# A graph attention layer on one core: two batches of edges per VectorE and ScalarE operation

## The chip, the core and the metric

One core of a Trainium2 chip runs the whole program. It has TensorE (PE; PEld is its weight load), VectorE (DVE), ScalarE (ACT), GpSimd (POOL) and SyncE (SP), each with a queue of its own that it works off in order, 16 DMA engines, the on-chip memories SBUF and PSUM, and HBM. The metric is the device time of one execution in microseconds.

## What is computed

6250 nodes with 256 channels, 100,000 edges sorted by destination, 8 heads of 32 channels. Cut to what matters:

```python
q, k, v = (feat @ W.T + b for W, b in ((Wq, bq), (Wk, bk), (Wv, bv)))      # by heads
score = clip(einsum('ehd,ehd->eh', q[dst], k[src]) / sqrt(32), -10, 10)
ex = exp(score - smax[dst]); alpha = ex / segment_sum(ex, dst)[dst]
wv = segment_sum(alpha[:, :, None] * v[src], dst)
x1 = feat + wv @ Wp.T + bp
h = layernorm(x1); h = gelu(h @ W1.T + b1) @ W2.T + b2                     # 1024 hidden
out = layernorm(feat + x1 + h)
```

## The kernel before

A prologue projects k and v of all nodes into rows in HBM (`kv_rows`), and q of the first 512. Then comes the stretch of the edges, and a tail for the last nodes.

**Edges.** A tile is 128 edges, a batch four tiles, a pair two batches (98 pairs, 196 batches). Eight batches are a turn (25 turns), and each engine runs its own `edges(turn, r, parity)`: a loop over the eight slots `i`, one batch a slot, in which the calls stand in the order of that engine's queue. Semaphores alone tie the engines together; the order is written out by hand. For batch `n`:

- POOL gathers four tiles of k and v rows by the edges' sources, one indirect DMA each (L362), into one of eight `kv` buffers, once `weight(n - 8)` has freed it (a wait on `s_ev`). In most turns one tile of slot 7 is not gathered but projected on TensorE from rows of x (`transpose_x`, `project_x`; an "x tile").
- PE, `q_rows` (L863): onehotT times the window of q rows gives q of each edge in `quad`, four PSUM banks, half of each used. It needs the products of the batch before, which free `quad`.
- DVE, `products` (L1463) and `scores` (L1470), `clip` (L1477): q times k, summed by head.
- ACT, `exponent` (L1108, L1109): exp into `bank5` and into `ev`.
- DVE, `weight` (L1483): v times exp into `ev`, two slots after its products (`weight(n - 2)` in slot n).
- PE, `sums` (L872): onehot times `ev`, added up in `bank4` over the pair.

By pair, and always in the same bank (`bank4`): ACT `stage` (L1117) copies the sums out, PE `merge` (L852) brings the four 32-row windows together, with a carry, ACT `copy_sums` (L1123) copies the result to `acc_sb`, SP `store_sums` writes it to HBM. `merge` and `copy_sums` stand one slot after `stage`. `sums` of the next pair waits for `copy_sums`. ACT also makes the transposed onehots two pairs ahead (L1094, L1099), DVE the onehots (L1449).

**Nodes.** Behind the edges run superblocks of 256 nodes, as `node_steps(turn, i)` spread over the slots of each engine: the sums' normalisation (`normalise`), `transpose_wv`, `project_out`, `residual`, norm, `transpose_h`, then one turn later `ffn1` in four parts with bias on ACT (L431), `gelu` (L436), `ffn2` in three parts, output. The gelu and the exp need different activation tables, so ACT loads one before and one after each gelu.

## Time and profile before

| | us |
|---|---|
| median of 3 runs | 1532.29 (1528.88 to 1538.81) |
| profiled execution, its own time | 1542.43 |
| its span, first to last instruction | 1540.6 |
| busy: PE / DVE / POOL / ACT | 1137.8 / 990.0 / 745.9 / 557.7 |
| POOL, 760 gathers of `kv` | 721.8 |

A span is what lies between an execution's first and last instruction. Busy time counts work, not waiting; the ends of matmuls are modelled, so a busy PE is not PE at its peak. A row of the trace names the line of the kernel, the engine and the tiles as out<-in. "idle before <-X" is how long the engine stood before this instruction, and whose update of a semaphore ended that. "issue" means that the profile shows no wait, "remote" that the update that ended the wait has no instruction near it in the profile. TensorE's granted clock is given as a share of 2.4 GHz, so 0.5 is 1.2 GHz.

### The profile page before, as it was taken

The numbers are of one execution on the slowest core, as the hardware profiler recorded it, in microseconds if no ns is written. First come the engines' busy times: TensorE is split into PE (matmuls) and PEld (weight loads), VectorE is DVE, ScalarE is ACT, GpSimd is POOL, SyncE is SP. The second block draws the span as 40 slices with busy tenths as digits, with TensorE's granted clock in tenths as the row PEclk, the third lists the DMA queues.
The fourth block names the chain that finished last, engine by engine and source line by source line (L and its number), as shares of the span: only waits on it lengthen the run. The fifth ranks groups of instructions, "written<-read, shape, count | busy, mean of one in ns | idle before, by whom it ended". The sixth has DMA issues, their size and how long they took to land.

```text
span 1540.6 us, 24484 instructions
## 1 busy us (share of the span) xinstructions
PE 1137.8 (74%) x6096; PEld 698.6 (45%) x6096; DVE 990.0 (64%) x1718; ACT 557.7 (36%) x1447; POOL 745.9 (48%) x800
## 2 busy tenths in 40 slices
PE   8924667776677688687668687788777877875887
PEld 7811234444344344444444444355444443443556
DVE  6824666675666676666566577667567666666673
ACT  2201223333234344334334344434334333333443
POOL 2364554554554554555545555445455544554400
PEclk9955668888888987888789888789788797798999
DMA  9975775765666666666656666656666665665510
GB/s 301 329 225 174 229 214 162 216 180 175 191 189 191 202 200 180 208 179 192 204 174 191 213 191 201 204 166 204 195 190 190 200 184 181 199 183 182 177 51 23
DMA packets 155387, 294.32 MB, mean 191 GB/s; under 512 B 32215, under 2 KB 92469, under 8 KB 155254
## 3 DMA queue, kind: packets, MB, share of 16 engines
q0 software_dynamic: 61856, 202.16, 43.8%
q1 hardware_dynamic: 93398, 90.90, 18.9%
q14 instruction: 112, 0.92, 0.2%
q8 instruction: 21, 0.34, 0.1%
HBM read 258.61 MB, written 34.34 MB: 190 GB/s over the span
## 4 chain that ended last, share of the span: by engine, by line
PE 26%; DVE 23%; another core or an unknown queue 23%; issue 21%; ACT 2%; DVEq 2%; SPq 2%; DMA 1%; POOL 0%; ACTq 0%; POOLq 0%
DVE score L1470 8%; DVE ev L1483 7%; PE quad L802 4%; PE bank L443 4%; PE bank L423 3%; PE quad L863 3%; PE bank L872 2%; DVE prod L1463 2%; PE bank L885 2%; DVE stats L453 1%; PE bank L852 1%; DVEq L1462 1%; PE bank L395 1%; PE bank L389 1%
## 5 line engine op out<-in xcount | busy, mean ns | idle before, releaser
L362 POOL DMA_INDIRECT kv<-kv_rows,src_sb x760 | 721.8, 950 | 658.7 <-DVE ev L1483 341.6
L1463 DVE TENSOR_TENSOR prod<-kv,quad 128x1024 f32<-128x1024 f32 x196 | 239.3, 1221 | 416.8 <-remote 333.3
L863 PE MATMUL quad<-qwin,onehotT 32*128 32x256 f32 x1568 | 167.3, 498 | 168.6 <-DVE prod L1463 107.3
L872 PE MATMUL bank<-ev,onehot 128*32 128x264 f32 x1568 | 150.2, 453 | 124.1 <-ACT acc_sb L1123 83.0
L1470 DVE TENSOR_REDUCE score<-prod 128x32 f32<-128x1024 f32 x196 | 238.0, 1214 | 2.4 <-DVE root L471 0.5
L1483 DVE TENSOR_TENSOR ev<-kv,bank 128x1024 f32<-128x1024 f32 x196 | 238.1, 1215 | 0.5 <-ACT ev L1109 0.5
L423 PE MATMUL bank<-hT,w_sb 128*128 128x256 f32 x736 | 215.3, 444 | 29.2 <-ACT hid L431 23.8
L863 PEld LDWEIGHTS quad<-qwin,onehotT 32*128 32x128 f32 x1568 | 73.2, 215 | 272.4 <-issue 177.9
L423 PEld LDWEIGHTS bank<-hT,w_sb 128*128 128x128 f32 x736 | 161.2, 225 | 76.3 <-issue 38.2
L443 PE MATMUL bank<-w_sb,hid 128*128 128x256 f32 x736 | 192.0, 414 | 0.1
L443 PEld LDWEIGHTS bank<-w_sb,hid 128*128 128x128 f32 x736 | 150.4, 210 | 29.9 <-issue 7.2
L431 ACT ACTIVATE hid<-bank,b_sb 128x256 f32<-128x256 f32 x184 | 77.1, 471 | 217.3 <-remote 126.9
L872 PEld LDWEIGHTS bank<-ev,onehot 128*32 128x32 f32 x1568 | 34.9, 116 | 199.5 <-issue 189.6
L1123 ACT ACTIVATE acc_sb<-bank 128x264 f32<-128x264 f32 x98 | 37.9, 386 | 238.3 <-remote 161.2
L852 PE MATMUL bank<-staged,place 128*128 128x264 f32 x196 | 81.9, 505 | 52.3 <-issue 30.2
L1108 ACT ACTIVATE bank<-clipped 128x32 f32<-128x32 f32 x196 | 38.5, 196 | 199.2 <-issue 125.6
L1117 ACT ACTIVATE staged<-bank 128x264 f32<-128x264 f32 x98 | 38.2, 389 | 181.5 <-remote 114.1
L852 PEld LDWEIGHTS bank<-staged,place 128*128 128x128 f32 x196 | 33.3, 213 | 91.8 <-issue 58.0
L395 PE MATMUL bank<-wp_sb,wvT 128*128 128x256 f32 x200 | 74.4, 536 | 0.0
L389 PE MATMUL bank<-bias_rows,one_rows 2*128 2x512 f32 (+1 forms) x120 | 63.6, 530 | 13.1 <-DVE x L401 12.4
L802 PE MATMUL quad<-wqkv_sb,xT_parts 128*128 128x512 f32 x288 | 66.4, 391 | 0.0
L802 PEld LDWEIGHTS quad<-wqkv_sb,xT_parts 128*128 128x128 f32 x288 | 54.3, 189 | 11.6 <-DVE xT_parts L1298 0.2
(128 smaller groups left out, 1176.3 us busy)
## 6 DMA issues: line engine op xcount, KB each, us to landing
dst_rows<-edge_dstT SPq DMA_DIRECT2D x50, 256.0 KB
qwin<-q_rows SPq DMA_DIRECT2D x392, 32.0 KB
kv_rows<-kv_out SPq DMA_DIRECT2D x24, 512.0 KB
kv<-kv_rows,src_sb POOLq DMA_INDIRECT x760
agg_rows<-acc_sb SPq DMA_DIRECT2D x98, 82.5 KB
xT_sb<-xT SPq DMA_DIRECT2D x25, 256.0 KB, 4.6
xq_sb<-xT SPq DMA_DIRECT2D x25, 256.0 KB
agg_in<-agg_rows SPq DMA_DIRECT2D x24, 264.0 KB
```

Source lines behind the costliest of these rows:

```text
L362: return nc.gpsimd.indirect_dma_start(out=rows, out_offset=None, in_=kv_dram, in_offset=bass.IndirectOffsetOnAxis(ap=index, axis=0))
L389: nc.tensor.matmul(rows, one_rows[:], bias_rows[:, cols], start=True, stop=False)
L395: last = nc.tensor.matmul(bank6[:, a * C:(a + 1) * C], wvT[:, (a * KC + k) * P:(a * KC + k + 1) * P], wp_sb[:, k * C:(k + 1) * C], start=F ...
L423: last = nc.tensor.matmul(bank[:, j * SB:(j + 1) * SB], w1_sb[:, k * HIDDEN + f * P:k * HIDDEN + (f + 1) * P], hT[:, k], start=(k == 0), s ...
L443: last = nc.tensor.matmul(bank[:, a * C:(a + 1) * C], hid[:, f, a * P:(a + 1) * P], w2_sb[:, f * C:(f + 1) * C], start=False, stop=(a == 1 ...
L802: last = nc.tensor.matmul(rows, lhsT, rhs, start=(n == 0), stop=(n == len(passes) - 1))
L852: nc.tensor.matmul(bank4[:, 0:ACC], place[:, slot % 2], staged[:, slot % 2], start=True, stop=True)\
L863: last = nc.tensor.matmul(quad[:, i, 0:C], onehotT[rows, slot // 2, cols], qwin[rows, slot // 2], start=True, stop=True)
L872: last = nc.tensor.matmul(bank4[WIN * i:WIN * (i + 1), 0:ACC], onehot[:, slot // 2, TILES * (slot % 2) + i, :], ev[:, slot % 4, i], start= ...
L1463: nc.vector.tensor_tensor(prod[:, slot % 2].rearrange("p (i c) -> p i c", c=C), kv[:, slot, :, 0:C], quad[:, :, 0:C], ALU.mult).then_inc(s ...
L1470: nc.vector.tensor_reduce(score[:, slot % 2], prod[:, slot % 2].rearrange("p (h d) -> p h d", d=HD), AX.X, ALU.add).then_inc(s_score, 1)
L1483: nc.vector.tensor_tensor(ev[:, slot % 4, :, 0:C].rearrange("p i (h d) -> p i h d", d=HD), kv[:, slot, :, C:2 * C].rearrange("p i (h d) -> ...
```

## The change

**By pair.** `quad` is used in full: `q_rows` fills it with q of eight tiles. `products`, `scores`, `clip`, `exponent` and `weight` each take a pair, with half as many instructions of twice the width. `ev` keeps its eight tiles' worth as two pairs; `prod`, `score` and `clipped`, which had two buffers of one batch, have one of a pair; `acc_sb` has two buffers instead of four. A pair's weighting frees both of its `kv` buffers, and `weight(p - 1)` stands in the slot of pair p.

**Order.** On PE `sums(p - 1)` come right behind `q_rows(p + 1)`, then a node step, then `merge(p - 1)`, in the slot of pair p. On ACT `exponent`, `stage` and `copy_sums` of pair p-1 all stand in this slot. The node chain moves one slot ahead (`normalise` 3 to 2, `project_out` 4 to 3, `residual` 5 to 4, and so on). The x tile of a turn goes to slot 1 of the next turn. The last turn has an order of its own (`last_edges`), in which the second FFN of an earlier superblock moves ahead, and the tail is reordered.

Core of the diff:

```diff
-        ev = sb("ev", [P, 4, TILES, ACC])
-        acc_sb = sb("acc_sb", [P, 4, ACC])
+        ev = sb("ev", [P, 2, PAIR_TILES, ACC])
+        acc_sb = sb("acc_sb", [P, 2, ACC])
...
-        prod = sb("prod", [P, 2, TILES * C])
+        prod = sb("prod", [P, PAIR_TILES * C])
...
                     if exists(n - SLOTS, BATCHES):
-                        pool.wait_ge(s_ev, n - SLOTS + 1)
+                        pool.wait_ge(s_ev, 4 * turn + (i // 2 - 3))
```

TensorE's `edges`:

```diff
-                for i in range(SLOTS):
-                    n = SLOTS * turn + i
-                    if exists(n + 1, BATCHES):
-                        q_rows(n + 1, (i + 1) % SLOTS, 4 * turn + (i + 1) // 2, turn + (i + 1) // SLOTS + 1)
-                    if i % 2 == 0 and exists(4 * turn + i // 2 - 2, PAIRS):
-                        merge(4 * turn + i // 2 - 2, (i // 2 + 2) % 4)
-                    if i != 5:
-                        node_steps(turn, i)
-                    if exists(n - 2, BATCHES):
-                        sums(n - 2, (i - 2) % SLOTS, 4 * turn + (i - 2) // 2)
-                    if i == 5:
-                        node_steps(turn, i)
...
+                for j in range(HALF_TURN):
+                    p = 4 * turn + j
+                    q_rows(p + 1, (j + 1) % 4, turn + (j + 1) // 4 + 1)
+                    if exists(p - 1, PAIRS):
+                        sums(p - 1, (j + 3) % 4)
+                    node_steps(turn, 2 * j)
+                    if exists(p - 1, PAIRS):
+                        merge(p - 1, j + 3)
+                    node_steps(turn, 2 * j + 1)
```

ScalarE's:

```diff
-                for i in range(SLOTS):
-                    n = SLOTS * turn + i
-                    if exists(n - 1, BATCHES):
-                        exponent(n - 1, (i - 1) % SLOTS)
-                    done = 4 * turn + i // 2 - 2
-                    if i % 2 == 0 and exists(done, PAIRS):
-                        copy_sums(done, (i // 2 + 2) % 4)
-                    if i % 2 == 0 and exists(done + 1, PAIRS):
-                        select_carry(done + 1, (i // 2 + 3) % 4)
...
-                    node_steps(turn, i)
-                    if i % 2 == 1 and exists(done + 1, PAIRS):
-                        stage(done + 1, (i // 2 + 3) % 4)
...
-                    if i % 2 == 0 and exists(4 * turn + i // 2 + 2, PAIRS):
-                        transposed_onehots(4 * turn + i // 2 + 2, (i // 2 + 2) % 4, turn + i // 4 + 1)
...
+                for j in range(HALF_TURN):
+                    p = 4 * turn + j
+                    if exists(p - 1, PAIRS):
+                        exponent(p - 1, j + 3)
+                        if j:
+                            node_steps(turn, 2 * j - 1)
+                        else:
+                            node_steps(turn - 1, 7)
+                        select_carry(p - 1, j + 3)
+                        stage(p - 1, j + 3)
+                    node_steps(turn, 2 * j)
+                    if exists(p - 1, PAIRS):
+                        copy_sums(p - 1, j + 3)
+                    late_steps(turn, 2 * j)
+                    if exists(p + 2, PAIRS):
+                        transposed_onehots(p + 2, (j + 2) % 4, turn + j // 2 + 1)
```

VectorE's:

```diff
-                for i in range(SLOTS):
-                    n = SLOTS * turn + i
-                    if exists(n - 1, BATCHES):
-                        clip(n - 1, (i - 1) % SLOTS)
-                    if exists(n, BATCHES):
-                        products(n, i, turn)
-                    if i % 2 == 0 and exists(4 * turn + i // 2, PAIRS):
-                        onehots(4 * turn + i // 2, i // 2)
-                    if exists(n - 2, BATCHES):
-                        weight(n - 2, (i - 2) % SLOTS)
-                    node_steps(turn, i)
-                    if exists(n, BATCHES):
-                        scores(n, i)
...
+                for j in range(HALF_TURN):
+                    p = 4 * turn + j
+                    if exists(p - 1, PAIRS):
+                        clip(p - 1)
+                    products(p, j, turn)
+                    onehots(p, j)
+                    if exists(p - 1, PAIRS):
+                        weight(p - 1, (j + 3) % 4)
+                    node_steps(turn, 2 * j)
+                    scores(p)
+                    node_steps(turn, 2 * j + 1)
```

`onehots(p)` waits for `exponent(p - 1)`, before as after. `late_steps` are the gelu (third pair of a turn) and `norm_h` (fourth).

How the queues read now. First ScalarE (ACT), from one `staged` copy to the second exponential after it, in the second and third slot of a turn (L431 is the FFN bias, L1132 the copy of projected q). Before:

```order
L1117 ACTIVATE staged<-bank 128x264
L1108 ACTIVATE bank<-clipped 128x32
L1109 ACTIVATE ev<-clipped 128x4x8
L1123 ACTIVATE acc_sb<-bank 128x264
L1126 ACTIVATE place<-carry_all 128x1
L1132 ACTIVATE q_next<-bank 128x512
L431 ACTIVATE hid<-bank,b_sb 128x256 x2
L1094 ACTIVATE distance<-dst_rows,minus_start 128x256
L1099 ACTIVATE onehotT<-distance,one_col 128x256
L1108 ACTIVATE bank<-clipped 128x32
L1109 ACTIVATE ev<-clipped 128x4x8
```

The same place now (L1162 is `stage`, L1168 `copy_sums`, L1153 and L1155 `exponent`, L448 the bias, L402 the copy of wvT):

```order
L1162 ACTIVATE staged<-bank 128x264
L402 ACTIVATE wvT<-bank 128x512
L448 ACTIVATE hid<-bank,b_sb 128x256 x2
L1168 ACTIVATE acc_sb<-bank 128x264
L1138 ACTIVATE distance<-dst_rows,minus_start 128x256
L1143 ACTIVATE onehotT<-distance,one_col 128x256
L1153 ACTIVATE bank<-clipped 128x64
L1155 ACTIVATE ev<-clipped 128x8x8
```

An exponential of one batch stood between `staged` and `acc_sb`; now none does, and the next one, for a whole pair, stands behind `acc_sb` and the transposed onehots.

Second, TensorE (PE) in the same slots (L389 and L885 project q, L423 is a quarter of the first FFN, L380 transposes wv). Before:

```order
L852 MATMUL bank<-staged,place 128x264
L423 MATMUL bank<-hT,w_sb 128x256 x4
L872 MATMUL bank<-ev,onehot 32x264 x4
L863 MATMUL quad<-qwin,onehotT 128x256 x4
L423 MATMUL bank<-hT,w_sb 128x256 x4
L389 MATMUL bank<-bias_rows,one_rows 128x256
L885 MATMUL bank<-wqkv_in,xq_sb 128x256 x2
L389 MATMUL bank<-bias_rows,one_rows 128x256
L885 MATMUL bank<-wqkv_in,xq_sb 128x256 x2
L872 MATMUL bank<-ev,onehot 32x264 x4
L863 MATMUL quad<-qwin,onehotT 128x256 x4
L852 MATMUL bank<-staged,place 128x264
```

Now, one pair (L880 is `q_rows`, L893 `sums`, L869 `merge`, L397 the transposes of wv, L440 the first FFN):

```order
L880 MATMUL quad<-qwin,onehotT 128x256 x8
L893 MATMUL bank<-ev,onehot 32x264 x8
L397 MATMUL bank<-ident,wv 128x128 x4
L440 MATMUL bank<-hT,w_sb 128x256 x4
L869 MATMUL bank<-staged,place 128x264
```

The sums of a pair stood behind a node step, and its merge behind the next q rows; now the sums stand at once behind the q rows, and a node step stands between them and their merge.

## Rows read from the trace of the kernel before

**Rows 1.** The page: span; busy us, share, instructions per engine.

```profile
span 1540.6 us, 24484 instructions
...
PE 1137.8 (74%) x6096; PEld 698.6 (45%) x6096; DVE 990.0 (64%) x1718; ACT 557.7 (36%) x1447; POOL 745.9 (48%) x800
```

**Rows 2.** Instructions on tile prod: ns min/median/max, first to last start.

```profile
L1463 DVE TENSOR_TENSOR prod<-kv,quad x196: 1214/1221/1224, 89.2 to 1479.7; 128x1024 f32<-128x1024 f32 x196
```

**Rows 3.** The waits: us in total, times, longest us.

```profile
POOL kv L362 <- DVE ev L1483: 341.6, 81, 9.1
DVE prod L1463 <- remote: 333.3, 75, 12.2
...
ACT acc_sb L1123 <- remote: 161.2, 31, 7.7
```

**Rows 4.** Timeline, 1351 to 1367 us: start, us, instruction, [idle before <-releaser].

```profile
1351.60 1.21 DVE L1483 TENSOR_TENSOR ev<-kv,bank 128x1024 f32<-128x1024 f32 x1
...
1353.59 0.94 POOL L362 DMA_INDIRECT kv<-kv_rows,src_sb  x1 [4.95 <-DVE ev L1483]
...
1355.18 0.66 PE L872 MATMUL bank<-ev,onehot 128*32 128x264 f32 x8
...
1355.90 0.39 ACT L1117 ACTIVATE staged<-bank 128x264 f32<-128x264 f32 x1 [0.35 <-PE bank L872]
...
1357.31 0.71 PE L852 MATMUL bank<-staged,place 128*128 128x264 f32 x2
...
1357.86 1.89 PE L423 MATMUL bank<-hT,w_sb 128*128 128x256 f32 x8
...
1362.61 0.95 POOL L362 DMA_INDIRECT kv<-kv_rows,src_sb  x1 [0.30 <-issue]
...
1363.77 1.22 DVE L1463 TENSOR_TENSOR prod<-kv,quad 128x1024 f32<-128x1024 f32 x1 [3.73 <-remote]
...
1365.32 0.39 ACT L1123 ACTIVATE acc_sb<-bank 128x264 f32<-128x264 f32 x1 [6.78 <-remote]
```

**Rows 5.** Groups of instructions: count, busy us, mean ns, idle us before <-releasers.

```profile
L362 POOL DMA_INDIRECT kv<-kv_rows,src_sb x760 | 721.8, 950 | 658.7 <-DVE ev L1483 341.6 <-issue 310.5 <-DMA kv_rows<-kv_out 6.6
...
L431 ACT ACTIVATE hid<-bank,b_sb 128x256 f32<-128x256 f32 x184 | 77.1, 471 | 217.3 <-remote 126.9 <-PE bank L423 65.3 <-issue 25.1
...
L1099 ACT ACTIVATE onehotT<-distance,one_col 128x256 f32<-128x256 f32 x98 | 49.8, 508 | 10.1 <-ACT distance L1094 1.4 <-issue 0.6
L1094 ACT ACTIVATE distance<-dst_rows,minus_start 128x256 f32<-128x256 int32 x98 | 49.5, 505 | 0.2
L436 ACT ACTIVATE hid<-hid 128x2048 f32<-128x2048 f32 (+1 forms) x24 | 44.2, 1840 | 0.3
L1109 ACT ACTIVATE ev<-clipped 128x32 f32<-128x32 f32 x196 | 42.0, 214 | 0.0
L1449 DVE TENSOR_TENSOR onehot<-dloc,bank 128x256 f32<-128x256 f32 x98 | 40.6, 415 | 3.8 <-ACT ev L1109 1.5 <-remote 1.5 <-issue 0.8
L1108 ACT ACTIVATE bank<-clipped 128x32 f32<-128x32 f32 x196 | 38.5, 196 | 199.2 <-issue 125.6 <-DVE ev L1483 73.3
...
L1123 ACT ACTIVATE acc_sb<-bank 128x264 f32<-128x264 f32 x98 | 37.9, 386 | 238.3 <-remote 161.2 <-PE bank L852 58.0 <-issue 19.0
...
L436 ACT ACT_TABLE_LOAD x23 | 29.5, 1283 | 0.4
...
L475 ACT ACTIVATE hn<-x,root 128x256 f32<-128x256 f32 x50 | 27.1, 589 | 4.4 <-DVE root L471 3.3 <-issue 0.7 <-DVE root L470 0.3
...
L401 DVE TENSOR_TENSOR x<-bank,x_in 128x512 f32<-128x512 f32 x24 | 16.5, 689 | 36.1 <-remote 18.1 <-issue 12.9 <-PE bank L395 5.0
```

**Rows 6.** Windows: us, busy per engine (PE to POOL), granted clock, DMA, GB/s.

```profile
640.00:697.00 57.00, 45.43 (x258) 27.31 (x257) 39.57 (x65) 24.27 (x65) 30.42 (x33) 0.88 0.65 194
80.00:136.00 56.00, 16.41 (x69) 7.79 (x73) 16.36 (x21) 4.87 (x16) 34.90 (x37) 0.51 0.66 197
```

**Rows 7.** Timeline after the edges, 1485 to 1500 us.

```profile
1490.97 7.17 PE L443 MATMUL quad<-w_sb,hid 128*128 128x256 f32 x32
```

More of the change, by code:

```diff
@@ L34 @@
 X_TILE = TILES - 1
-X_COPIED = {5: 3, 7: 6}
+EARLY_WORK, TURN_WORK = 1, 3
 EX_COL = 0
@@ L51, in configure @@
     LOOP_FROM = 6 if LOOPED else TURNS - 1
-    X_TILES = [(turn, i) for turn in range(TURNS) for i in x_slots(turn)]
+    X_FROM = 4 if LOOPED else TURNS
+    X_TILES = [x_target(turn, first) for turn in range(TURNS) for first in x_work(turn)]
     EDGE_COLS = BATCHES * TILES
@@ L68, in kv_halves, with x_work, x_target @@
     return 1 if u * SB + P >= NODES else 2
+def x_work(turn):
+    if not isinstance(turn, int) or X_FROM <= turn < LOOP_FROM + 2 * LOOPED:
+        return (TURN_WORK,)
+    return (EARLY_WORK, TURN_WORK) if turn < 2 else ()
+def x_target(turn, first):
+    return (turn, 7) if first == EARLY_WORK else (turn + 1, 1)
 def x_slots(turn):
-    if not isinstance(turn, int) or LOOP_FROM <= turn < LOOP_FROM + 2 * LOOPED:
-        return (7,)
-    return (5, 7) if turn < 2 else ()
+    if not isinstance(turn, int):
+        return (1,)
+    return tuple(i for t, i in X_TILES if t == turn)
 def x_index(turn, i):
@@ L647, in edges @@
                     n = SLOTS * turn + i
-                    done = 4 * turn + i // 2 - 2
+                    done = 4 * turn + i // 2 - 1
                     if i == 0 and exists(turn - 1, Q_UNITS - EARLY_Q):
@@ new lines, in last_edges @@
+            def last_edges(turn):
+                p, a, b = 4 * turn, turn - 2, turn - 1
+                q_rows(p + 1, 1, turn + 1)
+                ffn1(a, 0)
+                sums(p - 1, 3)
+                if exists(a - 1, SUPERBLOCKS):
+                    pe.wait_ge(f_z, a)
+                ffn1(a, 1, bank6)
+                merge(p - 1, 3)
+                pe.wait_ge(f_ev, 4 * a + 1)
+                ffn1_pair(2).then_inc(f_f1, 1)
+                sums(p, 0)
+                ffn1(a, 3)
+                merge(p, 0)
+                sums(p + 1, 1)
+                pe.wait_ge(f_ev, 4 * a + 2)
+                transpose_wv(b)
+                merge(p + 1, 1)
+                project_out(b)
+                pe.wait_ge(s_w2, 32)
+                pe.wait_ge(f_half, 1)
+                pe.wait_ge(f_x2, b + 1)
+                ffn2_part(range(FC // 2))
+                pe.wait_ge(f_gelu, a + 1)
+                ffn2_part(range(FC // 2, FC)).then_inc(f_f2, 1)
+                transpose_h(b)
@@ L1196, in node_steps @@
             def node_steps(turn, i):
-                ends = isinstance(turn, int) and turn == TURNS - 1
-                for j in x_slots(turn):
-                    if i == X_COPIED[j]:
-                        copy_x_kv(turn, j)
-                if i == 2 and exists(turn, Q_UNITS - EARLY_Q):
+                for first in x_work(turn):
+                    if i == first + 2:
+                        copy_x_kv(turn, first)
+                if i == 1 and exists(turn, Q_UNITS - EARLY_Q):
                     copy_q(turn)
-                if i + 4 in x_slots(turn):
-                    copy_x_rows(turn, i + 4)
@@ L1205, in node_steps @@
-                if i + 3 in x_slots(turn):
-                    copy_x_columns(turn, i + 3)
+                if i == 2 and exists(turn - 1, SUPERBLOCKS):
+                    copy_wv(turn - 1)
                 if i <= 3 and exists(turn - 2, SUPERBLOCKS):
                     ffn1_bias(turn - 2, i)
-                if i == 3 and exists(turn - 1, SUPERBLOCKS):
-                    copy_wv(turn - 1)
-                if i == 4 and not ends and exists(turn - 2, SUPERBLOCKS):
-                    gelu(turn - 2)
@@ new lines, in weight @@
+            def weight(p, slot, halves=(0, 1)):
+                first, last = halves[0], halves[-1] + 1
+                tiles = slice(first * TILES, last * TILES)
+                dve.wait_ge(s_exp, p + 1 + first)
+                nc.vector.tensor_tensor(ev[:, slot % 2, tiles, 0:C].rearrange("p i (h d) -> p i h d", d=HD),
+                                        kv[:, 2 * slot + first:2 * slot + last, :, C:2 * C]
+                                        .rearrange("p a i (h d) -> p (a i) h d", d=HD),
+                                        bank5[:, EX_COL + tiles.start * H:EX_COL + tiles.stop * H]
+                                        .rearrange("p (i h) -> p i h", h=H)
+                                        .unsqueeze(3).broadcast_to([P, tiles.stop - tiles.start, H, HD]),
```

383 lines of the change are left out of this document (234 added, 149 removed).

## The prediction

> **What bounds the kernel now.** I read the page first: no engine is full, TensorE is busy for 74% of the span and the clock is mostly granted [rows 1]. So the order of the handshakes sets the time, and the edge stretch is nearly all of it: the 196 `prod` products start between 89.2 and 1479.7 us [rows 2], 7.13 us apart, which is 57.05 us for a turn of eight batches and 14.3 us for a pair.
>
> Next the waits. VectorE stands 333.3 us before `prod` and ScalarE 161.2 us before `acc_sb`, both released by "remote", and POOL 341.6 us for the weighting on VectorE [rows 3]. "Remote" is a wait whose releaser the profile does not find near it. The timeline tells what it is [rows 4]. There the weighting of 1351.60 ends at 1352.81 and frees a buffer; POOL starts gathering 0.78 us later and issues eight gathers in a row, until 1363.56. Inside this burst TensorE ends two pieces that somebody waits for. The sums end at 1355.84, 2.25 us into the burst, and ScalarE's `staged` copy starts 0.06 us later. The merge ends at 1358.02, 4.43 us into the burst, and `acc_sb`, which waits for it (and for a store long past), starts at 1365.32, 7.3 us later and 1.76 us after the last gather. The product that starts at 1363.77 after a remote wait has waited for q rows in the same way. So I read: **a completion of TensorE passes early in a burst of gathers, and from about 3 us into it is held until 1 to 2 us after its end.** Where a chain crosses such a hold, gathering sets the time: 10 us of eight gathers, 1.76 us of release, then what VectorE must do until it frees buffers again. Two batches of the kernel before do this: 0.8 + 10.0 + 1.8 + a product and a weighting (1.1 + 1.2, overlapped) make 14.9, against the 14.3 measured.
>
> **The change, part by part.**
>
> *Fewer, larger VectorE operations.* Products, reductions and weightings go from 588 of 1024 elements to 294 of 2048. 512 elements take 0.689 us and 1024 take 1.215 to 1.221 [rows 2, 5], a slope of 1.03 ns an element, so 0.16 us is fixed: the double one takes 2.27 us and 294 x 0.16 = 48 us of busy time go. 98 clips go too, at the same fixed 0.16 us (my estimate for them): 16 us. VectorE waits 333 us before its products alone, so as long as something else sets the period, both are worth nothing. The Trainium skill has the rule for this (VectorE: DVE Perf Modes, on the TRN2 errata): the extra latency is paid per instruction, so one large tile pays it once. By that rule alone the kernel gains; the trace agrees with the fixed part, and what it would make of the time is a rival below.
>
> *ScalarE's exponentials* lose 98 pairs of 0.2 us; ScalarE is 36% busy: nothing.
>
> *TensorE* has the same matmuls. Nothing.
>
> *Gathers.* The same 760, but a pair's two batches are freed by one weighting, so each burst is eight gathers (seven with the x tile): 0.95 us and 0.30 us between them [rows 4, 5], 10.0 us for eight in [rows 4]. POOL alone then allows 10.0 + 0.8 = 10.8 us a pair.
>
> *The loop that closes.* Before, the weighting of a pair's second batch leads to its sums, `staged`, the merge one slot later and `acc_sb`; the next weighting that stands behind this `acc_sb` on ScalarE's queue is about three batches (21 us) on. Now sums, `staged`, merge and `acc_sb` of pair p-1 all stand ahead of the exponential of pair p, and the weighting of pair p needs that. One pair is the whole way round, with two completions of TensorE in it, and it starts with the same event that starts the burst. Queued behind the waiting `acc_sb` on ScalarE are the transposed onehots and the exponential; VectorE waits for that with its onehots and the weighting, POOL for the weighting, SP for `acc_sb` to store it.
>
> When the merge is held, weighting to `acc_sb` is 0.78 + 10.0 + 1.76 = 12.5 us, as [rows 4] have it. From there: `acc_sb` 0.39, distance 0.51, onehotT 0.51 and gaps, 1.5 together; exponentials 0.20 + 0.21 and a little for the double width, 0.5; onehots 0.41; the double weighting 2.27. That is 4.7, and the pair takes **17.2 us**. What the node steps put between on ScalarE comes on top [rows 5]: in the first pair of a turn a bias pair of 0.94 us half of the time, in the second the same always, in the third the gelu with two table loads (1.28 + 1.84 + 1.28 = 4.4), in the fourth `hn` (1.2). Held pairs: 17.6, 18.1, 21.6, 18.4.
>
> When it is not held, POOL's 10.8 us rules (VectorE needs 3 x 2.27 + 0.41 and its node steps, about 9), and in the third pair the gelu: 2.6 + 4.7 + 4.4 = 11.7.
>
> *Is it held?* The merge stands behind the sums and behind one node step. At full clock sums of eight tiles take 1.3 us (twice the 0.66 of [rows 4]), a quarter of the first FFN 1.89, the merge 0.71. From the weighting's end the merge is done after about 3.7 us in the first pair (2.9 into the burst, the edge of what passes; I take 0.6 for held), 4.6 in the second, where the transposed wv come first (3.8 into it; 0.9), 2.6 in the third (1.8; 0.3, since at half clock it would be 3 or more) and 4.8 in the fourth, with six matmuls of the second FFN at the pace of the first (4.0; 0.85). A mean share of 0.66.
>
> Sum of a turn: (0.6 x 17.6 + 0.4 x 10.8) + (0.9 x 18.1 + 0.1 x 10.8) + (0.3 x 21.6 + 0.7 x 11.7) + (0.85 x 18.4 + 0.15 x 10.8) = 14.9 + 17.4 + 14.7 + 17.3 = 64.3, less 1.0 for the burst of seven: 63.3. That is 6.2 more than 57.05, and 24 turns make **+150 us**.
>
> Bounds: with every merge held 75.7 - 1.3 = 74.4 us a turn, +416; with none 42.9, -340. In between a turn is about 42.9 + 31.5 x share, which meets 57.05 at a share of 0.45.
>
> *The clock* leans on the share. In 80 to 136 us, where TensorE is busy 16.4 of 56 us, it is granted 0.51, that is 1.2 GHz nearly throughout; in 640 to 697, busy 45.4 of 57, 0.88 [rows 6]. A held pair leaves TensorE idle for some 9 us, then the FFN piece starts at 1.2 GHz, takes twice 1.89 us, and the merge behind it is surely held. The Trainium skill says so too (TensorE: Matmul & The Clock Gate, in the table of why this matters for a kernel): an idle TensorE falls back to its half-rate clock. By it the share goes towards 1 and the time towards the upper bound; I keep 0.66, since TensorE stands for 6 us and more before this change too, and the window of 640 still has 0.88.
>
> *The tail.* The second FFN of superblock s-2, 7.17 us alone on the chain at 1490.97 [rows 7], moves in front of the last sums' follow-ups, where a part lies under VectorE's work: -7 us at the most likely, between -15 and +5, as the rest of the tail keeps its matmuls. The node chain one slot sooner has room both ways: nothing.
>
> Total: +150 - 7 = +143 on the profiled execution's own 1542.4 us (span 1540.6): 1685. The median of the runs is 10 us below that execution, so **1675 us**.
>
> **The rivals.**
>
> *A, chance 0.45, the forecast:* a share of 0.5 to 0.8, 1565 to 1790 us, most likely 1675.
>
> *B, nearly every merge held, 0.10:* cold clock, share over 0.8: 1790 to 1940.
>
> *C, faster, 0.26: the merges get out ahead of the gathers.* The place is the 3 us after a weighting, the price 6 to 10 us a pair, and the point from which it decides is the share of 0.45. For it: sums are now at once behind the weighting, and [rows 4] show a completion passing at 2.25 us; against it: every place but one has more than 2.5 us of TensorE work ahead of the merge. A share of 0.3 gives 52.4 us a turn, 24 x -4.7 = -112, less 7 and 10: 1413 us. Down to 0.2, 1340.
>
> *D, 0.10: only the operations' own fixed time counts.* If VectorE's queue sets the pace after all and the holds cost what they cost before, 48 + 16 us go and the tail's 7: 1460. It is the skill's rule from above. Against it speaks that VectorE idles for a third of the stretch.
>
> *E, even, 0.09:* a share near 0.45.
>
> **The numbers.** What a measurement of this kernel can tell from no change is about 1%. Slower by over 1%: A and B, 0.55. Within 1%: E, 0.09. Faster: C and D, 0.36. The likeliest case's own range is 1565 to 1790. The range for 8 in 10 takes in most of B and of C and all of D: 1400 to 1860.
>
> **What the profile after would show.** If right: `prod` starts further apart than 14.3 us a pair; bursts of eight gathers with 5 to 7 us of idle POOL between; ScalarE's wait before `acc_sb` by "remote" grown from 161 us to over 400, VectorE's large wait now before the onehots or the weighting and not before `prod`; a lower granted clock. If C: `acc_sb` starts within 4 us of the weighting's end in most pairs, POOL is hardly idle, and a pair takes 11 to 13 us. The forecast is wrong if holds depend on something other than the burst, or if the merge is done sooner than I count.

## The result, and the profile after

The changed kernel takes 1666.99 us (median of 4 runs, 1648.96 to 1700.14), the kernel before 1535.55 (4 runs, 1528.88 to 1554.32): 131 us more. The ratio, of fast executions alone (1649 and 1650 us against 1529 to 1539), is 1.076, 95% interval 1.067 to 1.084, or 116 us; the profiled execution below is the slowest of the four, so the main readings are set beside run 9, another profiled execution of the same kernel that took 1617 us. The forecast was 1675 us.

The profiled execution of the changed kernel has a span of 1698.3 us, 157.7 more than the one before [rows 1]. The page, its span and busy times:

```profile
span 1698.3 us, 22878 instructions
...
PE 1192.2 (70%) x6110; PEld 748.2 (44%) x6110; DVE 950.5 (56%) x1330; ACT 538.7 (32%) x1259; POOL 751.9 (44%) x800
```

VectorE is busy for 40 us less. TensorE is busy for 54 us more with nearly the same matmuls, since its clock is lower (below). Every engine's share has fallen: all wait more. The tile `prod` tells where (compare [rows 2]):

```profile
L1543 DVE TENSOR_TENSOR prod<-kv,quad x99: 1214/2287/2290, 95.2 to 1632.5; 128x2048 f32<-128x2048 f32 x97, 128x1024 f32<-128x1024 f32 x2
```

First to last product was 1390.5 us and is 1537.3: 146.8 of the 157.7 us lie in the edge stretch. Its start adds 6.0 us (95.2 against 89.2), the tail behind the last product 4.9 (65.8 against 60.9). Run 9 has the same start and tail (95.6 and 65.5) and 1454.2 us between its first and last product.

The waits (compare [rows 3]):

```profile
POOL kv L379 <- DVE ev L1569: 522.8, 60, 17.2
ACT staged L1162 <- remote: 302.5, 36, 15.7
...
DVE onehot L1526 <- ACT ev L1155: 272.4, 52, 10.3
DVE prod L1543 <- remote: 189.6, 28, 25.5
ACT q_next L1177 <- remote: 156.1, 17, 25.0
...
ACT acc_sb L1168 <- remote: 65.6, 18, 6.3
```

VectorE's wait before its products has shrunk from 333 to 190 us, and one of 272 us has come before the onehots, for ScalarE's exponential. But on ScalarE the wait by "remote" stands before `staged`, which needs the sums, and before `q_next`, which needs the projected q rows, and hardly before `acc_sb`, where I had put it. Run 9 has the same order: 210 us by "remote" before `staged`, 104 before `q_next`, 87 before `acc_sb`, 166 before `prod`, and 222 before the onehots. One held pair, the fourth of a turn, to be read against [rows 4] (start, us, instruction, idle before it):

```profile
650.66 2.28 DVE L1569 TENSOR_TENSOR ev<-kv,bank 128x2048 f32<-128x2048 f32 x1
...
653.09 1.10 PE L893 MATMUL bank<-ev,onehot 128*32 128x264 f32 x16 [1.16 <-issue]
...
653.73 0.95 POOL L379 DMA_INDIRECT kv<-kv_rows,src_sb  x1 [1.34 <-issue]
...
662.49 0.95 POOL L379 DMA_INDIRECT kv<-kv_rows,src_sb  x1 [0.30 <-issue]
...
665.44 2.29 DVE L1543 TENSOR_TENSOR prod<-kv,quad 128x2048 f32<-128x2048 f32 x1 [7.42 <-remote]
665.60 0.39 ACT L1162 ACTIVATE staged<-bank 128x264 f32<-128x264 f32 x1 [14.84 <-remote]
...
667.40 0.39 ACT L1168 ACTIVATE acc_sb<-bank 128x264 f32<-128x264 f32 x1 [1.42 <-PE bank L869]
```

The sums end at 654.19, 0.46 us into a burst of eight gathers that followed another after a pause of only 1.3 us; `staged` starts 11.4 us later, 2.2 us after the last gather. So early pieces are held too, here behind a short pause. And there is something that I had not seen in the trace of before. Another place, 28 us on, in a row of fifteen gathers (673.64 to 692.14):

```profile
682.65 0.11 PEld L893 LDWEIGHTS bank<-ev,onehot 128*32 128x32 f32 x1 [1.04 <-issue]
...
685.83 0.60 PE L893 MATMUL bank<-ev,onehot 128*32 128x264 f32 x1 [1.77 <-issue]
...
687.96 0.60 PE L893 MATMUL bank<-ev,onehot 128*32 128x264 f32 x1 [1.53 <-issue]
...
690.10 0.60 PE L893 MATMUL bank<-ev,onehot 128*32 128x264 f32 x1 [1.54 <-issue]
...
695.02 1.92 PE L893 MATMUL bank<-ev,onehot 128*32 128x264 f32 x10 [0.83 <-issue]
695.03 0.56 PEld L893 LDWEIGHTS bank<-ev,onehot 128*32 128x32 f32 x8 [0.61 <-issue]
695.04 0.60 ACT L1177 ACTIVATE q_next<-bank 128x512 f32<-128x512 f32 x1 [15.36 <-remote]
```

All inputs are there (the weighting ended at 682.54), yet TensorE gets through its first six matmuls one by one, up to 2.2 us apart, and runs the last ten within 1.9 us, from 2.9 us after the last gather on. Here not only its completions are late: it hardly gets to its next instruction.

From the trace I took, for pairs 8 to 91, the distance between the ends of successive weightings, and how long after a weighting `acc_sb` starts (over 8 us: held). The pairs of a turn are counted as in the prediction: the transposes of wv stand before the merge in the second, and the gelu behind `acc_sb` in the third.

| pair of a turn | period, forecast | measured | run 9 | held share, forecast | measured | run 9 | held / other pair, us |
|---|---|---|---|---|---|---|---|
| first | 14.9 | 13.1 | 12.7 | 0.60 | 0.29 | 0.38 | 19.7 / 10.4 |
| second | 17.4 | 19.4 | 18.5 | 0.90 | 0.86 | 0.76 | 20.7 / 11.3 |
| third | 14.7 | 15.6 | 13.9 | 0.30 | 0.33 | 0.14 | 21.6 / 12.6 |
| fourth | 17.3 | 15.6 | 14.5 | 0.85 | 0.76 | 0.57 | 17.1 / 10.9 |
| turn | 63.3 | 63.6 | 59.6 | 0.66 | 0.56 | 0.46 | |

The turn came out as forecast, and so did the order of its parts, except for the first pair, which is held half as often as I had put it. In run 9 there are fewer held pairs and the turn is 4 us shorter.

### The profile page after: what moved, and what is told of

The parts are those of the page before. It is cut to its first block and busy times, and to the rows that moved or that the text cites. A ratio compares the mean times of both kernels' runs of the same rounds, so it can differ in the third digit from the quotient of the medians.

```text
span 1698.3 us, 22878 instructions
## 1 busy us (share of the span) xinstructions
PE 1192.2 (70%) x6110; PEld 748.2 (44%) x6110; DVE 950.5 (56%) x1330; ACT 538.7 (32%) x1259; POOL 751.9 (44%) x800
## 5 line engine op out<-in xcount | busy, mean ns | idle before, releaser
L1543 DVE TENSOR_TENSOR prod<-kv,quad 128x2048 f32<-128x2048 f32 (+1 forms) x99 | 224.1, 2264 | 218.8 <-remote 189.6
L893 PE MATMUL bank<-ev,onehot 128*32 128x264 f32 x1568 | 201.7, 468 | 186.6 <-issue 134.8
L1526 DVE TENSOR_TENSOR onehot<-dloc,bank 128x256 f32<-128x256 f32 x98 | 41.3, 421 | 381.5 <-ACT ev L1155 272.4
L440 PE MATMUL bank<-hT,w_sb 128*128 128x256 f32 x736 | 220.1, 449 | 11.0 <-issue 10.1
L460 PE MATMUL bank<-w_sb,hid 128*128 128x256 f32 x768 | 219.3, 438 | 8.9 <-issue 8.3
L1569 DVE TENSOR_TENSOR ev<-kv,bank 128x2048 f32<-128x2048 f32 (+1 forms) x99 | 223.6, 2259 | 2.4 <-ACT ev L1155 2.4
L1553 DVE TENSOR_REDUCE score<-prod 128x64 f32<-128x2048 f32 (+1 forms) x99 | 223.5, 2257 | 0.8
L893 PEld LDWEIGHTS bank<-ev,onehot 128*32 128x32 f32 x1568 | 63.9, 121 | 301.1 <-issue 287.5
L440 PEld LDWEIGHTS bank<-hT,w_sb 128*128 128x128 f32 x736 | 164.8, 232 | 61.3 <-issue 29.5
L869 PE MATMUL bank<-staged,place 128*128 128x264 f32 x196 | 77.6, 484 | 139.1 <-ACT staged L1162 101.2
L1162 ACT ACTIVATE staged<-bank 128x264 f32<-128x264 f32 x98 | 38.3, 391 | 425.8 <-remote 302.5
L880 PE MATMUL quad<-qwin,onehotT 32*128 32x256 f32 x1568 | 127.9, 442 | 64.5 <-DVE prod L1543 25.8
L448 ACT ACTIVATE hid<-bank,b_sb 128x256 f32<-128x256 f32 x184 | 77.2, 471 | 231.6 <-PE bank L440 121.3
L880 PEld LDWEIGHTS quad<-qwin,onehotT 32*128 32x128 f32 x1568 | 79.7, 205 | 102.1 <-issue 97.8
L869 PEld LDWEIGHTS bank<-staged,place 128*128 128x128 f32 x196 | 39.8, 226 | 160.4 <-ACT staged L1162 112.6
L1168 ACT ACTIVATE acc_sb<-bank 128x264 f32<-128x264 f32 x98 | 38.3, 391 | 114.7 <-remote 65.6
L923 PE MATMUL bank<-wqkv_in,xgT 128*128 128x512 f32 x96 | 71.6, 887 | 0.0
L406 PEld LDWEIGHTS bank<-bias_rows,one_rows 2*128 2x128 f32 x123 | 25.7, 209 | 96.3 <-issue 74.6
```

Source lines behind the costliest of these rows:

```text
L406: nc.tensor.matmul(rows, one_rows[:], bias_rows[:, cols], start=True, stop=False)
L440: last = nc.tensor.matmul(bank[:, j * SB:(j + 1) * SB], w1_sb[:, k * HIDDEN + f * P:k * HIDDEN + (f + 1) * P], hT[:, k], start=(k == 0), s ...
L448: last = nc.scalar.activation(hid[:, f], bank[:, j * SB:(j + 1) * SB], ACT.Identity, bias=b1_sb[:, f:f + 1])
L460: last = nc.tensor.matmul(bank[:, a * C:(a + 1) * C], hid[:, f, a * P:(a + 1) * P], w2_sb[:, f * C:(f + 1) * C], start=False, stop=(a == 1 ...
L869: nc.tensor.matmul(bank4[:, 0:ACC], place[:, slot % 2], staged[:, slot % 2], start=True, stop=True)\
L880: last = nc.tensor.matmul(quad[:, i, odd * C:(odd + 1) * C], onehotT[rows, slot, odd * P:(odd + 1) * P], qwin[rows, slot], start=True, sto ...
```

## The experiments

The kernels ran in four groups, each on one chip with the kernel before between them. In two groups (chips numbered 3 and 1) it took 1509 and 1528 us, like in the result above: **condition A**. In the other two (numbered 14 and, later, 1 again) it took 1118 and 1120 us: **condition B**. Within a group the runs of the kernel before lie within 2.3% under A and 0.5% under B. Each kernel is compared with the kernel before of its own group.

**1. The merge out of the loop (A).**

```
 TensorE, pair p:                       ScalarE, pair p:
   q_rows(p + 1, ...)                     exponent(p - 1)
+  merge(p - 2, ...)                   +  copy_sums(p - 2)
   sums(p - 1, ...)                       stage(p - 1), node_steps(turn, 2 * j)
   node_steps(turn, 2 * j)             -  copy_sums(p - 1)
-  merge(p - 1, ...)                      transposed_onehots(p + 2)
```

> The change with one part undone: TensorE's merge and ScalarE's acc_sb copy of pair p-1 go back to the next pair's slot (merge(p-2) stands right behind the q rows, the copy right behind the exponential); everything else stays, the pairwise operations too. Theory 1 (holds close the loop): the loop from weighting to weighting then contains one completion of TensorE, that of the sums, which comes 1.2 to 2.1 us after the weighting and passes; the pairs that took 18 us and more mostly go, a pair takes 12.5 to 14.5 us, and the time is 1380 to 1560 us. Theory 2 (the time went into TensorE's instructions and the clock, not into the order): within 2% of 1667 us. Theory 3 (ScalarE's wait for the projected q rows, 156 us in the changed kernel, is the loss): at most 30 us faster than 1667.

Measured: 1699.0 us (4 runs), before 1528.1; ratio 1.116 (1.104 to 1.127). A pair takes 15.8 us, as in the changed kernel (15.9). Theory 1 misses by 139 us. The time lies in theory 2's range (within 2% of 1667), though runs 3 and 4 speak against TensorE's own work as the cause. The waits of this kernel:

```profile
DVE onehot L1530 <- ACT ev L1158: 358.2, 56, 11.8
ACT acc_sb L1171 <- PE bank L871: 303.1, 76, 7.7
...
ACT staged L1165 <- remote: 257.6, 49, 8.9
```

The sums' completion is still in the loop and is itself held, and the merge, now behind the q rows, has become a wait of its own. So this is no clean opening of the loop; it shows only that moving the merge alone gains nothing.

**2. The merge right behind the sums (A).**

```
 TensorE:                               ScalarE:
   sums(p - 1, (j + 3) % 4)               stage(p - 1, j + 3)
+  merge(p - 1, j + 3)                 +  copy_sums(p - 1, j + 3)
   node_steps(turn, 2 * j)                node_steps(turn, 2 * j)
-  merge(p - 1, j + 3)                 -  copy_sums(p - 1, j + 3)
```

> The changed kernel with the merge right behind its sums on TensorE (the node step behind it, not between) and the acc_sb copy right behind the staged copy on ScalarE. TensorE now idles about 1 us a pair for the staged copy, 97 us in all if nothing else moves. Theory 1 (what decides is whether the merge gets out before the burst of gathers): the merge ends 2.7 to 3.3 us after the weighting instead of 4.5 or later, fewer pairs are held, a turn falls from 63.6 to about 55 us, the time to 1420 to 1530 us. Theory 2 (completions are held wherever they fall in a burst, or TensorE gets its instructions slowly during one): 1640 to 1700 us. Theory 3 (no holds, TensorE's own time): up to 97 us slower, 1760.

Measured: 1751.9 us (4 runs, 1718.1 to 1791.6), before 1528.1: slower than the changed kernel. The second pair of a turn did what was hoped (merge 3.3 us after the weighting, 11.2 us a pair); the third, fourth and first took 18.6, 14.2 and 21.3. With that merge out early the loss came back in the pairs behind it: pairs of 16 us or more went from 37 to 42 of 84. By its time alone this fits theory 3 (up to 1760), but ScalarE's wait by "remote" before `staged`, 305 us, speaks for holds, and so for theory 2, whose range it misses by 52 us.

**3 and 4. Half the gathers, in both kernels (A).**

```
-  for t in range(tiles):                 # the four tiles of a batch
+  for t in range(tiles if turn == 0 else min(tiles, 2)):
       gather_rows(...)
```

> The changed kernel with two gathers per batch instead of four (from the second turn on; tiles 2 and 3 of a batch keep the rows of the first turn, so the result is not the reference's). A burst is four gathers, 5 us, not eight, 10 us. Theory 1 (a burst holds TensorE until 1 to 2 us after its end): a held pair is 0.8 + 5.0 + 1.1 + 4.7 = 11.6 us, the others 9 to 10, so about 10.5 x 97 + 160 = 1180 us, 1100 to 1260. Theory 2 (the chain of the operations itself, clock included, sets the pair): a pair stays at 15.9 us, 1600 us or more. Theory 3 (POOL's issue time is the bound): 10.8 x 0.5 = 5.5 us less a pair, 1130, but then POOL would be hardly idle.

> The same in the kernel before: two gathers per batch instead of four. Theory 1: bursts are shorter, the holds too, and VectorE becomes the bound at about 10 us a pair (990 us busy in all): 1080 to 1200 us. Then the changed kernel with half the gathers should be up to 64 us faster than this one (98 pairs x 4 fixed times of 0.16 us), since with short bursts the loop of one pair no longer costs. If the loop costs even without long holds, it stays slower than this one. Theory 2 (gathers are hidden): 1500 us or more.

Measured: the changed kernel 1254.0 us (2 runs), the kernel before 1120.5 (2 runs), ratios to the full kernel before 0.825 (0.815 to 0.835) and 0.737 (0.730 to 0.745). Engines' busy times, the changed kernel with half the gathers first, then the kernel before with half:

```profile
PE 1014.8 (81%) x6110; PEld 684.5 (54%) x6110; DVE 947.4 (75%) x1330; ACT 537.6 (43%) x1259; POOL 419.1 (33%) x449
```

```profile
PE 980.2 (88%) x6096; PEld 621.1 (55%) x6096; DVE 983.2 (88%) x1718; ACT 557.0 (50%) x1447; POOL 412.0 (37%) x446
```

Both kernels lose some 400 us with the gathers, more than the 330 us for which POOL is less busy, and TensorE has the same matmuls: gathering in bursts is what holds. But the gap between the two kernels stays, 133 us against 131, where fixed times alone would have made the changed one faster. The kernel before now gathers two at a time, and VectorE and TensorE are each busy for 88% of its span; the changed one gathers four at a time. I compared the end of each TensorE instruction that signals, inside a row of gathers less than 0.6 us apart, with the record of its semaphore's update, where there is one:

| kernel, condition | gathers in the row | late by, mean | over 1 us |
|---|---|---|---|
| before, half, A | 2 | 0.10 us | 2% |
| changed, half, A | 4 | 0.88 us | 37% |
| before, A | 4 | 1.3 us | 49% |
| before, A | 8 | 3.6 us | 68% |
| changed, A | 8 | 3.5 us | 68% |
| changed, order of run 5, B | 8 and more | 0.02 us | 0% |

At eight in a row both kernels are alike; but the kernel before has 52 rows of four and 40 of eight, the changed one 56 of eight, 13 of seven, ten of fifteen and none of four.

VectorE's and ScalarE's completions came 0.01 to 0.02 us late in all of them.

**5. The exponential ahead of the staged copy (B).**

```
 ScalarE, pair p:
   exponent(p - 1)
-  node_steps(turn, 2 * j - 1)
-  stage(p - 1), node_steps(turn, 2 * j), copy_sums(p - 1), late_steps(turn, 2 * j)
+  stage(p - 2), node_steps(turn, 2 * j - 2), copy_sums(p - 2), late_steps(turn, 2 * j - 2)
   transposed_onehots(p + 2)
+  node_steps(turn, 2 * j - 1)
```

> The changed kernel with ScalarE's exponential of pair p put ahead of its staged copy of pair p-1 (staged, the bias pairs and acc_sb follow it; the q copy follows too). The loop from one weighting to the next then contains no completion of TensorE on ScalarE's queue; they have one pair of slack, as before the change. All else is the changed kernel's, but TensorE's merge comes about 1 to 2 us later after its sums. Theory 1 (the closed loop through ScalarE is the loss): VectorE's wait for the exponential, 272 us, falls below 60, a pair takes 12.5 to 14.5 us instead of 15.9, the time is 1380 to 1560 us. Theory 2 (bursts of eight gathers hold TensorE longer than bursts of four, whatever the order): the wait moves to the products for q rows, a pair stays at 15 to 16.5 us, 1600 to 1700 us.

Measured: 1153.4 us (4 runs), the kernel before 1117.8; ratio 1.032 (1.029 to 1.035). The condition had changed, so the theories' ranges do not apply. What this run says is in comparison with the next two.

**6. The same with half the gathers (B).** The edits of 5 and of 3 together.

> The same order with two gathers per batch instead of four, so that the result is not the reference's. The changed kernel took 1254 us so, the kernel before 1121. Theory 1 (what is left with short bursts is the latency of the loop of one pair): 1050 to 1120 us, VectorE the bound at 9.1 us a pair. Theory 2 (the double operations or the clock cost it): 1200 to 1260 us.

Measured: 1150.3 us (2 runs), ratio 1.029 (1.024 to 1.033). Here half the gathers are worth 3 us, where under A they were worth over 400.

**7. Half the bytes (B).**

```
-  gather_rows(kv[:, i, t, :], ...)       # 2 KB a row
+  gather_rows(kv[:, i, t, 0:C], ...)     # 1 KB a row, from a table of 1 KB rows
```

> The changed kernel with gathers that fetch 1 KB for each row instead of 2 KB from the second turn on (as many gathers, half the bytes; the result is not the reference's). Theory 1 (the holds go with POOL's issuing of gathers): bursts last the same 10 us, holds too, 1560 to 1690 us. Theory 2 (the holds go with the bytes that the DMA engines still have to move): the holds shrink by half or more, 1180 to 1400 us.

Measured: 1151.9 us (2 runs), ratio 1.030 (1.027 to 1.033). Whether bytes or POOL's issuing hold TensorE can't be told where nothing is held, so that stays open. But this kernel is the changed one in all but the bytes, and it shows the sums and their `staged` copy, here of the third pair of a turn, without holds:

```profile
642.63 2.28 DVE L1569 TENSOR_TENSOR ev<-kv,bank 128x2048 f32<-128x2048 f32 x1
...
645.28 1.10 PE L893 MATMUL bank<-ev,onehot 128*32 128x264 f32 x16
...
645.69 0.94 POOL L379 DMA_INDIRECT kv<-kv_rows,src_sb  x1 [0.61 <-issue]
...
646.45 0.39 ACT L1162 ACTIVATE staged<-bank 128x264 f32<-128x264 f32 x1 [0.90 <-PE bank L893]
...
646.94 0.94 POOL L379 DMA_INDIRECT kv<-kv_rows,src_sb  x1 [0.30 <-issue]
```

`staged` starts 0.07 us after the sums, with POOL gathering almost without a break. A pair takes 10.2 us, the four of a turn 9.1, 9.4, 11.8 and 10.4.

In 5, VectorE's wait for the exponential (85.1 us in run 7) was gone. Of its three longest waits the one for the gathers is in run 7 too (29.7 us); those for `y_out` and the q rows are new:

```profile
DVE z L466 <- ACT y_out L492: 61.4, 21, 6.4
DVE prod L1552 <- DMA kv<-kv_rows,src_sb: 31.4, 5, 14.4
DVE prod L1552 <- PE quad L882: 31.1, 20, 3.3
```

**8. POOL stopped in mid-burst (B).**

```
+  if i % 2 == 1 and t == 0:
+      pool.wait_ge(s_mrg, ...)   # the merge of the pair that freed the buffers
   gather_rows(...)
```

> The changed kernel, with POOL stopped in the middle of each burst of eight: after four gathers it waits for the merge's completion of the pair whose weighting freed the buffers. Theory 1 (TensorE's completions are held while POOL gathers and released 1 to 2 us after): the merge gets out at the latest 0.8 + 5.0 + 1.1 = 6.9 us after the weighting instead of 12.5, the burst ends at 12, a pair takes 12.5 to 14 us, 1370 to 1520 us. Theory 2 (gathering time is what is missing, or completions are late for another reason): the idle POOL time is lost, 1680 to 1900 us.

Measured: 1169.4 us (5 runs), ratio 1.044 (1.042 to 1.047). Without holds the stop only costs.

**9. The changed kernel again (A).** No edit.

> The changed kernel once more, unaltered, because the four runs before this one came from a chip on which the kernel before takes 1118 us and not 1530, and on which TensorE's completions inside a burst of gathers came 0.02 us after their instructions. If the chip of this run is one where the kernel before takes about 1530 us: theory 1 expects 1630 to 1710 us and completions that come late. If it is one where it takes about 1118 us: by theory 1 (the loss of 132 us is the price of held completions) most of the loss is gone, and by the two kernels with less gathered data that ran there the changed kernel takes 1145 to 1165 us, 27 to 47 us more than before, all of it the loop's own latency (VectorE's wait of 85 us for the exponential).

Measured: 1639.6 us (4 runs), before 1509.4; ratio 1.075 (1.064 to 1.085), and completions inside rows of eight gathers 3.0 us late in the mean, 65% by over 1 us. Another group, the same picture.

**10. The exponential first, `y_out` early (A).**

```
   exponent(p - 1, j + 3)
+  if j == 0: norm_out(turn - 2)          # taken out of node_steps(turn - 1, 7)
   stage(p - 2, j + 2), ...               # the rest as in 5
```

> The order with the exponential first, and in addition ScalarE's second normalisation (y_out) put right behind the exponential that opens a turn, since VectorE waited 61 us for it there. Meant to beat both kernels. Where completions are not held: 1153 less up to 61 us, 1090 to 1130 us, against 1118 of the kernel before. Where they are held (kernel before about 1530): if the loop through ScalarE is the loss, 1380 to 1560 us; if the eight gathers in a row are, whatever the order, 1600 to 1700 us.

Measured: 1667.6 us (4 runs), before 1509.4; ratio 1.103 (1.095 to 1.111), in the group of run 9, which took 1639.6. The exponential no longer waits behind `staged` and `acc_sb`, and nothing is gained. VectorE's waits:

```profile
DVE prod L1554 <- remote: 412.2, 62, 25.2
DVE prod L1554 <- PE quad L882: 146.4, 13, 18.5
```

Before the onehots there is none left among the large ones; all of it stands before the products, for q rows. One burst's end in this kernel:

```profile
692.65 1.15 PE L882 MATMUL quad<-qwin,onehotT 32*128 32x256 f32 x16
...
699.26 0.95 POOL L379 DMA_INDIRECT kv<-kv_rows,src_sb  x1 [0.30 <-issue]
701.90 2.29 DVE L1554 TENSOR_TENSOR prod<-kv,quad 128x2048 f32<-128x2048 f32 x1 [5.91 <-remote]
...
704.10 0.41 DVE L1537 TENSOR_TENSOR onehot<-dloc,bank 128x256 f32<-128x256 f32 x1
...
704.43 2.28 DVE L1580 TENSOR_TENSOR ev<-kv,bank 128x2048 f32<-128x2048 f32 x1
...
707.50 0.94 POOL L379 DMA_INDIRECT kv<-kv_rows,src_sb  x1 [7.29 <-DVE ev L1580]
```

Last gather's end to release 1.7 us, then double product, onehots and double weighting, 4.8, then 0.8 to the first gather: 7.3 us of idle POOL, and with 10.0 us for eight gathers 17.3 us. The third and fourth pair of a turn take 16.6 and 17.0 here. The q rows that this product waits for were made at 692.65 to 693.80, with no wait of TensorE just before them, and the product started only at 701.90.

**11 and 12. The stop again, and the weighting split in two.** Meant for A, both fell into B.

> The changed kernel with POOL stopped after four gathers of each eight until the merge of the pair whose weighting freed the buffers is complete. It cost time on the chip where completions are not held (1169 us there, the kernel before 1118). Where they are held (kernel before 1510 to 1530, the changed kernel 1640 to 1667): theory 1 (the loss is the time that completions stand behind eight gathers in a row) expects the merge out at the latest 6.9 us after the weighting, 12.5 to 14 us a pair, 1370 to 1520 us. Theory 2 (POOL's lost gathering time adds to the pair): 1680 to 1900 us. On a chip without holds: 1160 to 1180 us again.

```
-  one weighting of the pair, 2048 elements
+  weight(p, slot, (0,)); weight(p, slot, (1,))    # 1024 each, each frees its batch
```

> The changed kernel with one part undone: each pair's weighting is two operations of 1024 elements again, each of which frees its batch's four buffers (products, sums, q rows and exponentials stay pairwise). The first gather of a burst starts 1.1 us sooner. Where completions are held: a held pair is VectorE's double product, onehots and weighting after the release and 12.6 us of burst and release before it, 17.6 us in all; if that is the chain, half to two thirds of the 97 pairs get 1.1 us shorter, 50 to 70 us in all, so 1570 to 1620 us, 3 to 4% below the changed kernel; if buffers are not what a pair waits for, 1640 to 1670 us. Where they are not held: 98 more fixed times of 0.16 us on VectorE, 1150 to 1170 us.

Measured: 1172.1 us (4 runs; ratio 1.047, 1.043 to 1.051), the first stop's time again, and 1154.2 us (4 runs; 1.029, 1.026 to 1.033). What they do where completions are held is not known.

No kernel of these that does the whole computation beats the kernel before, under A or B.

## Why the prediction was right, and where it was not

**That gathering holds TensorE: right, shown.** Under A, halving the gathers took 1667 to 1254 us and 1528 to 1121; under B it was worth 3 us (runs 5 and 6). But it is not the program alone that does it: under B the same rows of gathers hold nothing. What makes A or B is open; the chip's number does not tell, since 1 showed both.

**The size of a pair: right.** Held pairs were put at 17.6, 18.1, 21.6 and 18.4 us and take 19.7, 20.7, 21.6 and 17.1. Pairs that are not held were put at 42.9 us a turn; run 7, where none is, takes 40.7. The formula gives 60.5 us a turn for the measured share of 0.56, against 63.6, and 57.4 for run 9's 0.46, against 59.6.

**Which pairs are held: right for three of four.** The second, third and fourth pair came close to their shares; the first was put at 0.60 and is 0.29. The periods are off by -1.8, +2.0, +0.9 and -1.7 us, which nearly cancels: that the turn is off by only 0.3 us is luck, and in run 9 it is off by 3.7.

**What holds them: wrong in part.** The step said that the sums pass and that the merge's age in the burst, with an edge at about 3 us, decides. In the trace of before this edge is there. In the changed kernel nearly half of the early completions are late too. TensorE's completions inside rows of seven or eight gathers, those late by over 1 us, by the row's age when they were due:

| age | before | changed | run 9 |
|---|---|---|---|
| under 2 us | 5 of 56 | 40 of 84 | 38 of 96 |
| 2 to 3 us | 18 of 32 | 14 of 18 | 12 of 21 |
| over 3 us | 137 of 143 | 94 of 106 | 110 of 121 |

So of 47 held pairs 32 had `staged` start over 8 us after the weighting, before the merge could begin, and in only 15 did `acc_sb` start over 2 us behind the merge. Two terms were missing. ScalarE copies the projected q rows ahead of the second pair's `staged`, and that completion was held too (156 us in 17 waits, over 3 us in 14 of the 18 held second pairs); I had counted only bias pairs there. And I took each burst as starting afresh, where it goes with the pause before it: of the 25 bursts that began less than 2.5 us after the last gather, 24 gave a pair of 16 us or more, of the other 59 only 13 (run 9: 20 of 26, and 7 of 58). Of the 25 short pauses 15 stand in second pairs, but the others show it too (9 of 10). A pair that is not held leaves no pause: 25 of 37 such pairs are followed by a long one. No run changed the pause alone, so that it is the cause is not shown.

**The loop through ScalarE, as the cause of the loss: failed.** The step said that the next weighting must now wait for the merge and `acc_sb` of the last one, and that this closes a loop that was open before. The waits did move as it said (onehots 3.8 to 382 us idle, `prod` by "remote" 333 to 190). But with ScalarE's part opened the time did not fall (run 10: 1668 against 1640), and the loss then stood before `prod`, for q rows that were held themselves. Moving the merge did not help either (runs 1 and 2, 1699 and 1752), though these are no clean test. What the runs suggest is that under A each pair needs some completion of TensorE inside the burst, and that it hardly matters which.

**What stands in its place.** Part is shown: the changed kernel frees the buffers of eight gathers at once and the one before of four, and the longer the row of gathers, the later TensorE's completions (table in runs 3 and 4; with rows of two next to nothing is late, and the kernel before with half its gathers takes under A what the full one takes under B, 1121 and 1118 us). The changed kernel with half its gathers, in rows of four, takes 1254 us under A, about 100 more than its nearest kernels take under B. The rest is worked out, not shown: after a release VectorE must now do 4.8 us before the next buffer is free (run 10), where a single product and weighting were 2.4 [rows 2, 4], 2.4 us more in each held pair; with 0.56 of 97 pairs that is 130 us, with run 9's 0.46 it is 107. That takes the number of held pairs as unchanged, which no run shows, and with the 34 us below it comes to more than the loss. Splitting the weighting would have tested it, and fell into condition B. So what share of the loss each of the two has stays open.

**What is left without holds.** Under B the changed kernel itself was not run; runs 7 and 12, each but one step from it, take 1152 and 1154 us, 3% over the kernel before. There VectorE waits 85 us for the exponential (run 7), more than the 40 us that its operations save. So by these two, some 34 of the 131 us have nothing to do with held completions. Opening the loop there exchanged that wait for others and gained nothing (run 5), so this cause is narrowed down, not settled.

**The fixed time of an operation** was right (2.29 us, the median of a double product, 2.27 forecast), and worth nothing, as forecast: VectorE's busy time fell by 40 us, less than the 64 that I had counted. **The clock** fell a little, not to the floor: over the middle of the edge stretch 0.80 against 0.84, and 0.83 in run 9.

```profile
300.00:1500.00 1200.00, 858.61 (x4455) 525.94 (x4454) 678.33 (x894) 404.18 (x947) 560.83 (x590) 0.80 0.58 171
```

**The tail** was put at -7 us and is +4.9. The second FFN starts 16.2 us after the last product (11.3 before) and runs alone, as in [rows 7]. The step that failed is that it would move in front: in the last turn's order the transposes of wv and the projection now stand between the last sums and it. The projection ran at half clock, 3.78 us against 1.99 before, and run 9 shows the same:

```profile
1643.66 3.78 PE L412 MATMUL bank<-wp_sb,wvT 128*128 128x256 f32 x8
...
1648.71 7.17 PE L460 MATMUL bank<-w_sb,hid 128*128 128x256 f32 x32
```

**The signs.** Products further apart, VectorE's wait before the onehots, more idle POOL and a lower clock came as listed. ScalarE's wait before `acc_sb` of over 400 us did not: it fell to 66, and the "remote" waits stand before `staged`, `q_next` and `prod`. This sign spoke against the step on what holds the pairs.

## What to carry over

A merged operation also merges what it releases: before doubling one, count how many transfers start at once, and not only the fixed cost that it saves. A wait that the profile names shows where a loss lands, not what makes it: open it in one kernel and see whether the time moves or only the wait. A limit read from one kernel's trace, like the 3 us here, need not hold in the changed one. And times should be taken in more than one group of runs, with the kernel before in each, before a cause is called the kernel's own.

## What was not expected of the hardware

- The kernel before took 1509 to 1536 us in some groups of runs and 1118 to 1120 in others. What differs in the traces is TensorE's completions inside rows of GpSimd gathers: 3.0 us late in the mean in the one, 0.02 us for the kernels profiled in the other, with the gathers themselves nearly as long (950 ns, and 958 in run 5). VectorE's and ScalarE's are late in neither.
- The same traces differ in one thing more. Under A part of the engines' semaphore updates have no record (ScalarE in the changed kernel: 660 records for 947 updates), under B there are about as many records as updates (run 5: 950). So A and B may differ in how an execution is recorded; no run tells whether lost records and held completions have one cause.
- How late they are goes with the length of the row: 0.10 us for two gathers in a row, 0.9 to 1.3 for four, 3.5 to 3.6 for eight, all under condition A (3.0 in run 9).
- In such a row TensorE also gets to its instructions slowly: matmuls of 0.6 us came up to 2.2 us apart, and ten ran in 1.9 us once it had ended.
